# A perceiver layer: self attention and experts written into the program of the cross attention

## The reference

```python
def reference(x, ctx, ...):      # x (4, 128, 512), ctx (4, 2048, 512)
    # 16 heads of 64, softmax over the 2048 rows of ctx
    x = x + xattn(layernorm(x), ctx, ctx, Wq, bq, Wk, bk, Wv, bv, Wo, bo)
    # 16 heads of 32, qkv = x @ qkv_w.T + qkv_b, q and k and v times head_mask
    x = x + attn(layernorm(x), head_mask, qkv_w, qkv_b, fc_w, fc_b)
    x = x + ffn(layernorm(x), sim_matrix, gates, q_proj, k_proj, v_proj, o_proj)

def ffn(h, ...):                 # 16 experts, head size 128
    logits = l2norm(h) @ l2norm(sim_matrix) - sigmoid(gates)
    rw = softmax over the experts with logits > 0 (the best two where there are none)
    q, k, v = (einsum('btc,ech,bte->bth', h, w, rw) for w in (q_proj, k_proj, v_proj))
    ao = softmax(causal(q @ k.T / sqrt(128))) @ v
    return einsum('bth,ehc,bte->btc', ao, o_proj, rw)
```

## Time and profile before

| | us |
|---|---|
| median of 3 runs | 1491.55 (1487.49 to 1493.58) |
| the profiled execution | 1486.79 |
| its span, first to last instruction | 1484.9 |
| TensorE busy | 1436.0 |
| VectorE busy | 740.1 |
| ScalarE busy | 493.5 |
| GpSimd busy | 173.1 |

### The profile page before, as it was taken

The page is one execution under the profiler, slowest core; times in us unless marked ns, Lnnn a source line. Parts: engine busy times, 40 slices in busy tenths (PEclk is TensorE's granted clock), DMA queues, the critical chain, the costliest instruction groups (busy, mean ns, idle before and its releaser), DMA issues. The chain is left out here.

```text
span 1484.9 us, 22236 instructions
## 1 busy us (share of the span) xinstructions
PE 1436.0 (97%) x8564; PEld 1123.5 (76%) x8564; DVE 740.1 (50%) x1644; ACT 493.5 (33%) x1111; POOL 173.1 (12%) x150
## 2 busy tenths in 40 slices
PE   6999999999999999999999999999999699799999
PEld 4667788777777777787777777877887577688777
DVE  5335543463355335634443464345335555577779
ACT  3215531372154216512431372134214425411111
POOL 1321100130020003100100140011000113100012
PEclk9999999999999999999999999999999888899999
DMA  6511100240020004201100150010002230023200
GB/s 212 170 44 29 43 12 1 61 143 12 0 79 12 11 9 121 84 2 39 41 22 1 53 149 12 1 61 15 5 5 114 44 114 1 30 85 112 87 29 29
DMA packets 45366, 77.78 MB, mean 52 GB/s; under 512 B 8160, under 2 KB 16384, under 8 KB 43728
## 3 DMA queue, kind: packets, MB, share of 16 engines
q1 hardware_dynamic: 43616, 71.33, 15.3%
q0 software_dynamic: 1648, 5.04, 1.1%
HBM read 71.11 MB, written 5.24 MB: 51 GB/s over the span
## 5 line engine op out<-in xcount | busy, mean ns | idle before, releaser
L416 PE MATMUL b_ps<-b_ctxT,wk 128*128 128x512 f32 x1536 | 390.4, 403 | 0.0
L394 PE MATMUL b_ps<-wv,b_ctxT 128*128 128x512 f32 x1536 | 371.9, 401 | 12.7 <-DVE b_ctxT L594 12.7
L394 PEld LDWEIGHTS b_ps<-wv,b_ctxT 128*128 128x128 f32 x1536 | 288.7, 190 | 89.0 <-issue 24.0
L416 PEld LDWEIGHTS b_ps<-b_ctxT,wk 128*128 128x128 f32 x1536 | 281.7, 188 | 87.9 <-issue 25.9
L575 ACT COPY b_pT<-b_ps 128x512 f32<-128x512 f32 x128 | 74.8, 585 | 610.7 <-PE b_ps L445 610.1
L685 DVE COPY b_pT<-b_ps 128x512 f32<-128x512 f32 x128 | 88.3, 690 | 267.1 <-PE b_ps L445 266.9
L607 DVE COPY b_V<-b_ps 128x512 f32<-128x512 f32 x128 | 88.4, 691 | 246.0 <-PE b_ps L394 246.0
L569 ACT ACTIVATE b_prob<-b_prob,b_negm 128x512 f32<-128x512 f32 x256 | 182.9, 720 | 59.4 <-DVE b_negm L706 59.4
L700 DVE TENSOR_SCALAR_CACHE_REDUCE b_prob<-b_ps 128x512 f32<-128x512 f32 x256 | 166.5, 688 | 30.6 <-PE b_ps L432 29.3
L445 PEld LDWEIGHTS b_ps<-ident,b_prob 128*128 128x128 f32 x1024 | 119.3, 140 | 19.4 <-issue 2.5
L445 PE MATMUL b_ps<-ident,b_prob 128*128 128x128 f32 x1024 | 132.9, 272 | 0.7 <-ACT b_pT L575 0.7
(11 more groups left out here) (201 smaller groups left out, 1217.2 us busy)
## 6 DMA issues: line engine op xcount, KB each, us to landing
stage<-in_ctx SPq DMA_DIRECT2D x64, 256.0 KB, 3.0
b_wo<-in_Wo SPq DMA_DIRECT2D x8, 1024.0 KB, 6.6
stage<-in_Wk SPq DMA_DIRECT2D x30, 256.0 KB, 2.7
stage<-in_Wv SPq DMA_DIRECT2D x28, 256.0 KB, 3.2
b_q<-q_s SPq DMA_DIRECT2D x32, 128.0 KB, 3.1
w_rows<-in_self_w SPq DMA_DIRECT2D x4, 1024.0 KB, 8.2
w_tiles<-in_q_proj SPq DMA_DIRECT2D x16, 256.0 KB, 3.9
w_tiles<-in_k_proj SPq DMA_DIRECT2D x16, 256.0 KB, 3.4
```

The costliest lines, as they stand in the source:

```text
L394: mm = nc.tensor.matmul(ps[:, bank], ctxT[:, a, k, n * P:(n + 1) * P], wv[:, w, k], start=m == 0, stop=m == len(terms) - 1)
L416: mm = nc.tensor.matmul(ps[:, bank], wk[:, i % 2, w, k], ctxT[:, a, k, s * BANK:(s + 1) * BANK], start=m == 0, stop=m == len(terms) - 1)
```

## The change

All three parts become one block, `layer`. A new class `Tail` holds the work of self attention and experts as items, named by two or three letters and digits: `sx` transpose of the normed batch, `sq` `sk` `sv` its projections, `tq` `tk` transposes of queries and keys, `sl` logits of a unit, `sr` its division, `sp` its transposes, `sw` weighing, `sf` output product with the next layer norm, `sh` transposes of that, `sim` and `gl` and `gc` the gating (now in two groups of two batches), `wt` the split of expert weight tile m, `y` an expert product, `eq` `es` `ee` `en` `ep` `ea` the experts' attention, `eo` an output product. Each engine walks through the same list in its order and does its part of each item. Some items stand in the steps 114 to 135 of the cross attention (`TAIL_STEPS`), the others behind it (`TAIL`, then `experts()`: y of tiles 4 to 11 and the 64 `eo`). The batches go in the order 0, 1, 3, 2.

Products take a PSUM bank from one queue of banks; behind the cross attention all 8 are in it. Projections of queries and keys now have tokens on the partitions, and each is transposed for the logits. The logits of a batch are 16 matrix products that alternate over the four row quarters, into four banks. Square roots of layer norm and gating are replaced by `root`, an integer first guess and three Newton steps on VectorE. 20 of the 64 output products (`by_act`) are scaled by ScalarE, 4 of them into `alt` and 16 into one of four tiles `part`; GpSimd adds these 16 and, once for each batch, `x` to `alt`; VectorE takes up `alt` at the first product of tile 15. The rest parts of weight tiles 0, 1, 2, 13, 14, 15 are GpSimd's. The self attention's weights go through the staging tiles of the context, split like a fifth batch; the expert weights go to three tiles of 1 MB over the freed values.

```diff
+TAIL_STEPS = {114: "lr0", 115: "lr1", 116: "lr2", 117: "lr3", 119: "lr4", 120: "gate", 121: "ln0 sx0", 122: "ln1", 123:
+              "sx1", 124: "ln2", 125: "sx2", 131: "sk0", 133: "sq0 tq0", 134: "sv0 sq1 const tk0", 135: "sk1"}
+TAIL = """sl00 sl01 sl02 tk1 sr00 sr01 sv1 tq1 sp00 sl03 sr02 sx3 sp01 sl10 sq3 sr03 sr10 sp02 sl11 sk3 sp03 sp10 tq3 tk3 cs sw0 sv3 sl12
+sl13 sr11 sr12 sq2 wt0 sf0 sp11 sl30 sr13 sl31 sk2 sr30 sp12 sp13 sp30 sw1 sl32 sl33 sr31 sr32 sv2 tq2 sh0 sf1 sr33 sp31 tk2 wt1
+sl20 sr20 sh1 sl21 sp32 sp33 sl22 sim sw3 wt2 gl0 sr21 sr22 gc0 y00 sf3 sl23 sp20 sp21 y01 sr23 y10 sp22 y11 sp23 sw2 sf2 y20
+sh3 wt3 sh2 y21 gl1 gc1 y30 y31 y03 wt4 y02 y13 y12 y23 wt5 wt6 y22 y33 y32"""
...
+        at = {x: n for n, x in enumerate(self.rest)}
+        def place_one(x):
+            if x in at:
+                banks.remove(soonest := min(banks, key=lambda bank: at.get(last[bank], -1)))
+                banks.appendleft(soonest)
+            bank = banks.popleft()
+            banks.append(bank)
+            self.bank[x], self.earlier[x], last[bank] = bank, last.get(bank), x
...
+    def by_act(self, item):
+        return item[3] == 1 and item[1] < 15 or item[3] == 3 and item[1] < 14
...
+    def experts(self):
+        rest = []
+        follow = {(4, 0): [("wt", 7)], (5, 0): [("wt", 8)], (6, 0): [("wt", 9)], (7, 0): [("wt", 10)], (8, 0): [("wt", 11)],
+                  (8, 1): [("eq", 0), ("eq", 1)], (8, 3): [("es",)], (9, 0): [("wt", 12)], (9, 1): [("ee",)], (9, 3): [("en",)],
+                  (10, 0): [("wt", 13)], (10, 1): [("ep",)], (11, 0): [("wt", 14)],
+                  (11, 1): [("ea", SELF_ORDER[0])], (11, 2): [("ea", SELF_ORDER[1])], (11, 3): [("ea", SELF_ORDER[2])]}
+        for m in range(4, 12):
+            for n, b in enumerate(SELF_ORDER):
+                rest += [("y", m, b)] + follow.get((m, n), [])
+        outs = [("eo", m, b, e) for m in range(12, 16) for pair in (SELF_ORDER[:2], SELF_ORDER[2:]) for e in range(EG) for b in pair]
+        for n, x in enumerate(outs):
+            rest += [x] + [("ea", SELF_ORDER[3])] * (n == 1) + [("wt", 15)] * (n == 2)
+        return rest
...
+        elif kind == "eo" and item in G.sums:
+            b, n = item[2], G.sums[item]
+            if n > 1:
+                pool.wait_ge(self.sum_done, n - 1)
+            if G.by_act(item):
+                pool.wait_ge(self.scaled_done, G.nth_act[item])
+                more = self.part[:, G.parts.index(item) % 4]
+            else:
+                pool.wait_ge(self.out["eo"], G.nth_add[item])
+                more = X.xs[:, b]
+            nc.gpsimd.tensor_tensor(self.alt[:, b], self.alt[:, b], more, ALU.add).then_inc(self.sum_done, 1)
...
+        for r in range(R):
+            bank_free(("sl", b, r))
+        for g in range(R):
+            for r in range(R):
+                rows = slice(r * HD, (r + 1) * HD)
+                mm = self.nc.tensor.matmul(self.bank(("sl", b, r))[:, g * P:(g + 1) * P], self.qT[rows, k % 2, g], self.kT[rows, k % 2, g],
+                                           start=True, stop=True)
+                if g == R - 1:
+                    mm.then_inc(self.psum["sl"], 1)
...
+        elif kind == "eo" and G.by_act(item):
+            _, m, b, e = item
+            w, k = (m - 12) * EG + e, G.rank[b]
+            act.wait_ge(self.psum[kind], nth)
+            to = self.alt[:, b]
+            if item in G.parts:
+                n = G.parts.index(item)
+                to = self.part[:, n % 4]
+                if n >= 4:
+                    act.wait_ge(self.sum_done, G.sums[G.parts[n - 4]])
+            nc.scalar.activation(to, self.bank(item), ACT.Copy, scale=self.rw[:, k, w:w + 1]).then_inc(self.scaled_done, 1)
...
+    def root(self, dve, x, y, part):
+        V, E = self.nc.vector, x.shape[-1]
+        bits, near, minus = self.bits[:, :E], self.near[:, :E], self.minus[:, :E]
+        if part == 0:
+            V.tensor_scalar(minus, x, -0.5, None, ALU.mult)
+            self.step(dve, V.tensor_scalar(bits, x.bitcast(I32), 1, None, ALU.logical_shift_right))
+            self.step(dve, V.tensor_scalar(y.bitcast(I32), bits, -1, 0x5F3759DF, ALU.mult, ALU.add))
+        else:
+            self.step(dve, V.tensor_tensor(near, y, y, ALU.mult))
+            self.step(dve, V.tensor_tensor(near, near, minus, ALU.mult))
+            self.step(dve, V.scalar_tensor_tensor(y, near, 1.5, y, ALU.add, ALU.mult))
...
+        elif kind == "sf":
+            b = item[1]
+            dve.wait_ge(self.psum[kind], nth)
+            dve.wait_ge(self.fb_done, nth)
+            V.tensor_tensor(X.xs[:, b], self.bank(item), X.xs[:, b], ALU.add).then_inc(self.out[kind], 1)
+            dve.wait_ge(self.out[kind], nth)
+            self.step(dve, V.bn_stats(stats[:, b], X.xs[:, b]))
+            self.step(dve, V.bn_aggr(mv[:, b], stats[:, b]))
+            self.step(dve, V.tensor_scalar(self.var2[:, b:b + 1], mv[:, b, 1:2], EPS, None, ALU.add))
+            for n in range(4):
+                self.root(dve, self.var2[:, b:b + 1], self.rstd2[:, b:b + 1], n)
+            if nth >= 2:
+                dve.wait_ge(self.psum["sh"], nth - 1)
+            V.tensor_scalar(self.xn2[:], X.xs[:, b], mv[:, b, 0:1], self.rstd2[:, b:b + 1], ALU.subtract, ALU.mult).then_inc(self.xn2_done, 1)
...
+            if (m, e) == (15, 0):
+                dve.wait_ge(self.sum_done, G.merge_of(b))
+                rows = self.alt[:, b]
+            V.scalar_tensor_tensor(X.xs[:, b], self.bank(item), self.rw[:, k, w:w + 1], rows, ALU.mult, ALU.add
+                                   ).then_inc(self.out[kind], 1)
...
+                    if b == NB - 1:
+                        tail.vector(dve, X, ("ln", b))
...
-        cross_attention(nc, Z, M, x, ctx, Wq, bq, Wk, bk, Wv, bv, Wo, bo, q_s,
-                        lambda sp, part: load_rows(sp, Z, M, self_w, part))
-        self_attention(nc, Z, M, head_mask, qkv_b, fc_b, gates, projections)
-        expert_attention(nc, Z, M, sim_matrix, projections, out)
+        layer(nc, Z, M, x, ctx, Wq, bq, Wk, bk, Wv, bv, Wo, bo, q_s, self_w, qkv_b, fc_b, head_mask, head_maskT, gates,
+              sim_matrix, projections, out)
```

1375 lines of the change are left out of this document (691 added, 684 removed).

## The result

The changed kernel takes 1480.88 us in the median of 5 runs (1480.16 to 1482.49), beside 1490.43 for the one before in the same comparison (1487.49 to 1493.58): a ratio of 0.9937, 95% interval 0.9922 to 0.9952. The time lies inside the range, just under its upper end, and the direction is right. But less than half of the gain arrived: between the profiled executions (1486.79 and 1480.88) it is 5.9 us.

The account below looks back on a forecast made before the run. TensorE was taken as the bound, with waits and low clock after the cross attention. Stage 3 -35.1, stage 2 +14.1, stage 4 -3.2 and stage 5 0 gave -24.2 from 1486.8: forecast 1463 us, range 1446 to 1481.

Parts of the forecast that it names:

- Stage 3, the work: Cross attention's last output product to expert tile 3's end: TensorE's work 110.6 us, with logits' alternation saving 6.0.
- Stage 3, the waits: Same stretch: the old 21.2 us of TensorE waits go, four others totalling 14.4 come.
- (a): Behind the last output product TensorE waits 1.5 us for the first probabilities, ready about 8.4 us after the start.
- (b): In stage 3, `sh1` waits for the chain of `sf1`: 1.7 us with the copy of `tk2`.
- (c): From the end of `sim`, unit 2,1's division stands behind the first gating: 13.8 us against TensorE's 8.9, wait 4.9.
- (d): From `sp23` to `gl1` each item needs the one before: waits of 6.3 us together.
- Stage 2: Where the cross attention runs out: takes up 17.0 us of moved work, loses 2.9 idle us, +14.1.
- Stage 4: Expert tiles 4 to 11: expert weights' rests no longer stand ahead of q and v reductions, -3.2 us.
- Stage 5 and the additions: The 64 output products: no change from 48.3 us; GpSimd's additions at 1.3 us finish in time, 2.7 to spare.
- The mutual exclusion at 1475: Last stage: VectorE and GpSimd exclude each other, 56 us instead of 43.6; milder form of the additions rival (0.03).
- The clock: Stage 3: 7 us lost to TensorE's low clock instead of 17, mean clock 0.93 or more.
- VectorE becomes the bound: Rival, chance 0.12: VectorE's 115 us of work make stage 3 150 us, the time 1481.

Follow-up runs that it names:

- logits_rowwise: Changed kernel with the logits' loops exchanged, so four products of one row quarter stand together and nothing alternates: 1480.26 us, 0.9945 of the kernel before.
- rests_moved: Changed kernel with GpSimd's rest part of tile 0 placed where no square root runs, and that of tile 2 given to VectorE: 1475.43 us.
- combined: Changed kernel with rests_moved, weights_bias, h_swapped, later small loads, batch 0's norm a step earlier, three divisions earlier, and batch 2's value projection moved: 1465.05 us.
- weights_bias: Changed kernel with the self attention's weights split two pieces a step (steps 125 to 133), bias loads ahead of the last eight pieces: 1474.62 us.
- h_swapped: Changed kernel with the high part and the rest of the experts' input exchanging places in SBUF: 1479.22 us, 0.9933 of the kernel before.
- two_steps: Changed kernel with two Newton steps instead of three in the roots behind the cross attention: 1481.72 us, 0.9947 of the kernel before.

## Why the prediction was right and wrong

- **What bounds, and what the change removes**: right. The two waits of 4.79 and 4.30 us, each at a block's start, are gone, and stage 3 is 28.3 us shorter.
- **Stage 3, the work**: 117.6 forecast with the clock, 114.5 measured. Inside it the logits were mis-sized: 0.65 from the scores, 2.8 us a batch, measured 1.10. Alternation brings 2.72 to 1.10 and grouping 4.32 to 2.72. The Trainium skill ("TensorE: Matmul & The Clock Gate", Part 3, measured speedup) gives 3.07 times for four row tiles of 512 columns; here, with 128 columns, alternation alone gives 2.5 and the whole is 4.32 / 1.10 = 3.9. What alternation gave was worth nothing, as logits_rowwise shows: it was returned in waits, because VectorE was behind. By an estimate, with the logits at 1.10 the sum of the work is 110.6 - 4 x 1.7 = 103.8, so some 10.7 of the 114.5 us are the low clock and what else that sum had too small, not 7.
- **Stage 3, the waits**: the step that failed, 14.4 us forecast, 24.3 measured.
  - (a) The first probabilities came 8.4 us after the start, as I wrote (1200.35 to 1208.74), but TensorE had only 5.0 us of work ahead of them, since its logits were short: 3.41 instead of 1.5.
  - (b) 2.01, forecast 1.7.
  - (c) 4.75, forecast 4.9: luck. With the collision away (rests_moved) it is 0.54. There VectorE and GpSimd need 12.8 us from `sim` to the product of unit 2,1 (1261.79 to 1274.57), where I had 13.8; but TensorE has not 8.9 but 12.8 us of work ahead of it (1261.38 to 1274.18), because its clock is at 0.68 there (12.8 x 0.68 = 8.7). The collision then added 4.3 to the chain and filled what the slow TensorE had covered. (The 6.0 us for "the whole gating" end at L1344, as the earlier trace rows does, and that is not its last instruction; for this term it was the right place, since the division stands there.)
  - (d) 1.43 + 1.51 + 1.55 = 4.5, forecast 6.3.
  - Not in the sum at all is the wait of 4.91 behind the norm chain of batch 0, of which 2.7 are the collision (2.22 without).
- **The cause that I didn't see**: I moved rest parts of 4.6 us on GpSimd beside roots of small SBUF instructions on VectorE, and priced both alone. The section "SBUF: two separate sides" of the Trainium skill's "SBUF — State Buffer" has the rule: a GpSimd instruction and a VectorE instruction exclude each other for a whole instruction if VectorE's runs in a mode that uses two ports, or if VectorE's has two SBUF inputs and GpSimd's reads SBUF. The trace agrees: the multiplication at 1233.94 has two SBUF inputs and took 2.85 us, up to GpSimd's end, while reads from PSUM went on. The one of 4.49 us is a `tensor_scalar` of two elements per partition with one SBUF input; one of a single element (0.15 us at 1233.50) was not held. By the rule the first would be in a two-port mode, which no run here shows by itself; but it was held a second time, in combined, where it takes 0.97 us at 1255.57 and ends with GpSimd's divisions (1256.51). The collision itself is shown without the rule: with GpSimd's rest parts away from the roots, the same two instructions take 0.16 and 0.17 us, and the time falls (rests_moved). I had weighed the rule against the 20 additions, whose VectorE partner reads PSUM, and not against the roots.
- **Stage 2**: "takes up the 17.0 us moved and loses 2.9 idle us". 1.3 us of the moved work stand in stage 1 (three transposes of 0.42), which leaves 15.7. No idle time was covered; 5.6 us stand there instead of 2.9, 2.7 more. TensorE's busy time grew by another 1.7, and the clock fell to 0.56 from 1162 to 1168. Together that is the 20.1 measured. The last output product of the cross attention stands 24.6 us later (1199.31), not 14. The step that failed here: I moved the weights' splits with the batch logic and counted no VectorE or ScalarE time for them, in the only steps that have no value product beside them. weights_bias shows it, -4.9 us.
- **Stage 1**: "unchanged". 1.3 us are the transposes, 1.33 a wait for VectorE's norm, which stood directly ahead of its reader (one step earlier it is gone), 1.2 the scatter of the start; the rest is small.
- **Stage 4**: -3.2 forecast, -2.1: the idle time went as forecast, but an expert product is 2.77 and not 2.72. The place of the two input tiles in SBUF has a part in it, as h_swapped shows; the rest is open.
- **Stage 5 and the additions**: right, 48.35 for 48.3, 1.29 for 1.3 us, no wait for `alt`. The mutual exclusion at 1475 didn't happen.
- **The clock**: 7 us forecast. Not separable from the work by a run, 10.7 by the estimate above; the mean is 0.88 and was to be 0.93 or more. Of the three signs of being wrong, a clock that "stays at 0.87" came true but for 0.01; idle time over 30 us did not (24.3), and the last stage is as long as before.
- **The rivals**: 1481 for "VectorE becomes the bound" is nearly the measured time, and its stage 3 (115 us of work in 150) is not: VectorE has 103 in 138.8, and 7 of them are collision. As a mechanism it is half right: TensorE's 6.5 us were free (logits_rowwise), and 4.0 us less of VectorE's work came back as clock (two_steps, 103.0 to 99.0 us).

## What to carry to other kernels

When work moves onto GpSimd, list what VectorE runs at the same time, and check each instruction for SBUF inputs; a chain of tiny ones is a bad partner, since one of them can wait for nearly the whole of the long one. When a wait shows an idle engine as its releaser, follow it to what that engine waited for. And price every engine's part of a moved item: the sum of TensorE's work in stage 3 was right to 3 us, though by terms that missed in both directions, and most of what was lost came from parts of VectorE, ScalarE and GpSimd that had no term.

## What the runs showed of the hardware

- A VectorE instruction of 0.17 us took 4.49 us beside a GpSimd rest part of 4.55, and one of 0.16 took 2.85 beside one of 4.58; with both rest parts away from there the kernel was 5.5 us faster (4.6 by the ratios).
- 32 entries of 32 x 128 matrix products: 4.32 us in four groups among other work, 2.72 in one group by quarter, 1.10 alternating over four quarters.
- Four matrix products with one stationary tile take 0.93 or 0.91 us, and the difference went with the tile's place in SBUF when the places were exchanged.
- TensorE's clock can take back what shorter waits give: where five waits had become 0.6 to 0.8 us shorter (two_steps), it was at 0.68 instead of 1.00 from 1294 to 1304, and the time stayed. The same 24 products took 7.21 us behind a break of 2.94, 7.39 behind 2.21 and 5.82 behind 1.99.
